# Attention rows from columns by a unit matrix, maxima three heads ahead, GpSimd's last bias after the columns

## The chip, the cores and the metric

The kernel runs on one core of a Trainium2 chip. The metric is the device time of one execution in microseconds. Three runs of the kernel before gave 1441.47, 1442.12 and 1445.12 us; their median is 1442.12.

## The reference

Five blocks, each with a residual and a layer norm where the reference has them, work on 625 nodes with 768 features and 10,000 edges. The first two (relational and plain graph convolution) are untouched. The change concerns the graph attention layers, all of this form:

```python
def gat(x, W, a_src, a_dst, bias, src, dst, heads, c):
    h = (x @ W).reshape(n, heads, c)
    al_s, al_d = einsum(h, a_src), einsum(h, a_dst)      # one number per node and head
    e = leaky_relu(al_s[src] + al_d[dst], 0.2)
    e = exp(e - segment_max(e, dst)[dst])
    alpha = e / (segment_sum(e, dst)[dst] + 1e-16)
    return segment_sum(h[src] * alpha, dst) + bias
```

There are four: a residual block with 4 heads of 256 (layer A, `Q0`) and 1 head of 768 (layer B, `Q1`), both with self loops, and a block with 8 heads of 96, then ELU (`Q2`), and 1 head of 768 (`Q3`), whose output gets the residual and the last layer norm.

## The kernel before, in words

Edges are held as dense count matrices of 625 by 625, in 5 blocks of 125 nodes. Every engine has its own program, written out by hand in order; they meet only by counting semaphores. TensorE multiplies features and weights in split precision: a block of work is 3 products (high by low, low by high, high by high). The weights come in chunks of 128 rows, which ScalarE splits into a high part and GpSimd into the rest (`split_hi`, `split_to`).

A feature product has two pieces of 384 columns. The first piece also gives each node's two attention numbers, `al`. The second runs block by block (`chunks_and_scores`, 30 blocks, 40 in layer B), and a table of events (`PAIR_EVENTS`) says before which block TensorE does something for the scores. For a head h:

1. `turn_scores` (once a layer) turns `al` into rows; ScalarE copies them.
2. `send_row` gives every partition the row of source numbers in banks 5 and 6, or 2 and 3.
3. `largest`, five times: VectorE adds the mask of a block and takes the maximum.
4. `columns`: six small VectorE operations make, for each destination, the two numbers of leaky relu minus maximum, "steep" and "flat", each as a high and a low part (`row_parts`).
5. `turn_columns`: five TensorE turns make rows of them; `keep_columns`: ScalarE copies these in two operations.
6. `send_columns`: products with a stationary operand of two ones give every partition the flat and the steep row (with one pad column, 626).
7. `keep_flat`: ScalarE copies the flat row to SBUF; the steep row stays in PSUM.
8. `score`, five times on VectorE: the larger of steep row plus source number and flat row. ScalarE takes the exponential, `finish` on VectorE multiplies by the counts. In heads 1 to 7 of the eight-head layer the last three tiles (`LATE = 3`) go to ScalarE in two steps each and to GpSimd for the counts (`late_products`).
9. `sum_head` (or `sum_tile`): TensorE sums the features with these tiles.

In the eight-head layer the second piece is followed by a loop over the heads. TensorE, in turn h: row of head h+2, send of head h+1, sum of head h, turn of head h+2's columns. VectorE: inverse of head h-1, products of head h, maxima and columns of head h+2, scores of head h+1. ScalarE: the read of head h-1, flat row and exponentials of head h+1, ELU of head h-1. GpSimd: late products of head h+1, bias of head h, ELU sum of head h-1. In front of the last head TensorE turns the first half of the next layer's input. In the last layer GpSimd adds the bias to the residual (`x_residual`, five operations, L1046) as soon as its row is loaded.

Lines: `largest` L2204, `columns` L2213 to L2221, `score` L2253, `finish` L2260, inverse L2271 and L2273, `turn_columns` L2968, `send_columns` L2980, `send_row` L2960, `sum_head` L3061, the last layer's sums L3033 (first block) and L3011, `keep_flat` L1321, late products L1019, layer B's additions L974 (GpSimd) and L2317 (VectorE).

## Time and profile before

| | us |
|---|---|
| median of three runs | 1442.12 |
| profiled execution, its own time | 1445.38 |
| its span, first to last instruction | 1443.5 |
| TensorE busy | 1373.3 (95%) |
| VectorE busy | 775.4 (54%) |
| GpSimd busy | 548.4 (38%) |
| ScalarE busy | 445.3 (31%) |

Times in rows are microseconds from the start of the span. The second piece of layer B runs from about 1115 to 1139, that of the eight-head layer from 1241 to 1260, its heads from there to 1358, the second piece of the last layer from 1376 to 1401, and its sums to the end. Busy time of TensorE counts pipelined products by their whole duration, so a line of 0.34 us can follow the one before it by 0.18 us. `[5.72 <-ACT ...]` behind a row is the idle time before it and who ended it. In the names POOL is GpSimd, ACT ScalarE, DVE VectorE, PE TensorE.

### The profile page before, as it was taken

Reading aid. Unit: us, or ns where it says so; the run is one execution under the profiler, and the core shown is the slowest. Engines: PE = TensorE matmul, PEld = TensorE weight load, DVE = VectorE, ACT = ScalarE, POOL = GpSimd, SP = SyncE. Lnnn points to the kernel's source line nnn. Section 1 sums busy time; section 2 is a strip of 40 time slices with the busy share of each in tenths; the row PEclk is TensorE's granted clock in tenths of the full one; section 3 lists DMA queues with packets and bytes.
Section 4 is the critical chain, followed back from the end, with each engine's and each line's share of the span. In section 5 each row is a group of like instructions: output and inputs, shape, how many; then the busy total and the mean of one; then the engine's idle time right before and its main releaser. Section 6 shows DMA issues by size and latency. Waiting matters only on the chain.

```text
span 1443.5 us, 22327 instructions
## 1 busy us (share of the span) xinstructions
PE 1373.3 (95%) x7674; PEld 1275.8 (88%) x7674; DVE 775.4 (54%) x1843; ACT 445.3 (31%) x953; POOL 548.4 (38%) x626
## 2 busy tenths in 40 slices
PE   5999999999999999999999999999999999878997
PEld 3676999999999999999999999999978976767974
DVE  7876755234444356573232535764464615499554
ACT  1564521111100010110110312244574434557631
POOL 8000325234253434434342443144333654427630
PEclk9999999999999999999999999999999999977999
DMA  3101111113343223241121211122001311200001
GB/s 117 55 29 34 39 34 55 44 39 113 95 119 92 66 93 110 82 140 58 55 66 33 88 45 51 44 88 78 29 23 44 110 44 39 77 1 1 1 11 54
DMA packets 57802, 86.47 MB, mean 60 GB/s; under 512 B 6467, under 2 KB 54458, under 8 KB 57583
## 3 DMA queue, kind: packets, MB, share of 16 engines
q1 hardware_dynamic: 45204, 65.82, 15.3%
q10 hardware_dynamic: 12504, 19.36, 4.4%
q8 instruction: 63, 1.03, 0.3%
q14 instruction: 31, 0.25, 0.1%
HBM read 83.24 MB, written 1.92 MB: 59 GB/s over the span
## 4 chain that ended last, share of the span: by engine, by line
PE 79%; DVE 12%; ACT 3%; issue 2%; POOL 2%; DMA 1%; DVEq 0%; SPq 0%; ACTq 0%; POOLq 0%
PE psum L2499 13%; PE psum L2503 13%; PE psum L2502 13%; PE psum L2516 7%; PE psum L2519 7%; PE psum L3011 5%; DVE max_scratch L2204 3%; PE psum L2648 3%; PE psum L2573 2%; PE psum L3061 2%; PE psum L2912 1%; PE psum L2542 1%; PE psum L2545 1%; PE psum L2916 1%; PE psum L2917 1%
## 5 line engine op out<-in xcount | busy, mean ns | idle before, releaser
L2499 PE MATMUL psum<-w_lo,xT_hi 128*125 128x384 f32 (+4 forms) x1110 | 377.5, 340 | 3.8 <-POOL w_lo L926 1.8
L2503 PE MATMUL psum<-w_hi,xT_hi 128*125 128x384 f32 (+4 forms) x1110 | 373.4, 336 | 0.0
L2502 PE MATMUL psum<-w_hi,xT_lo 128*125 128x384 f32 (+4 forms) x1110 | 373.3, 336 | 0.0
L913 POOL CAST w_hi<-w_raw 128x384 fp32r<-128x384 f32 x190 | 105.1, 553 | 569.6 <-PE psum L2503 466.0
L1098 ACT ACTIVATE h_hi<-psum 125x384 fp32r<-125x384 f32 (+1 forms) x120 | 59.1, 492 | 529.3 <-PE psum L2503 524.9
L1754 DVE TENSOR_TENSOR h_lo<-psum,h_hi 125x384 fp32r<-125x384 f32 (+1 forms) x120 | 67.0, 558 | 286.6 <-ACT h_hi L1098 285.8
L2499 PEld LDWEIGHTS psum<-w_lo,xT_hi 128*125 128x125 f32 (+1 forms) x1110 | 205.9, 186 | 6.5 <-POOL w_lo L926 3.4
L915 POOL TENSOR_TENSOR w_lo<-w_raw,w_hi 128x384 fp32r<-128x384 f32 x190 | 201.1, 1059 | 15.2
L2502 PEld LDWEIGHTS psum<-w_hi,xT_lo 128*125 128x125 f32 (+1 forms) x1110 | 206.4, 186 | 0.4
L2503 PEld LDWEIGHTS psum<-w_hi,xT_hi 128*125 128x125 f32 (+1 forms) x1110 | 206.0, 186 | 0.0
L2516 PE MATMUL psum<-h_lo,adjacency 125*125 125x384 f32 (+3 forms) x600 | 203.5, 339 | 2.1 <-issue 1.9
L2519 PE MATMUL psum<-h_hi,adjacency 125*125 125x384 f32 (+3 forms) x600 | 202.8, 338 | 0.0
L926 POOL TENSOR_TENSOR w_lo<-w_raw,w_hi 128x384 fp32r<-128x384 f32 x86 | 89.7, 1074 | 92.4 <-ACT w_hi L1295 92.4
L2516 PEld LDWEIGHTS psum<-h_lo,adjacency 125*125 125x125 f32 (+1 forms) x600 | 111.4, 186 | 3.1 <-issue 2.7
L2519 PEld LDWEIGHTS psum<-h_hi,adjacency 125*125 125x125 f32 (+1 forms) x600 | 111.7, 186 | 0.0
L3011 PE MATMUL psum<-features,score_tiles 125*125 125x257 f32 (+2 forms) x380 | 107.6, 435 | 0.0
L3011 PEld LDWEIGHTS psum<-features,score_tiles 125*125 125x125 f32 x380 | 70.5, 189 | 27.8
L1936 DVE CUSTOM_DVE_ANT_0 score_products<-score_w_raw,score_a_rows 128x384 f32<-128x384 f32 (+2 forms) x116 | 57.5, 541 | 7.1 <-DMA score_w_raw<-weights_dram 3.4
L1897 DVE SCALAR_TENSOR_TENSOR x_nat<-psum,inv_degrees,x_nat 125x384 f32<-125x384 f32 x100 | 54.3, 610 | 11.8 <-PE psum L2519 11.7
L1701 DVE TENSOR_SCALAR onehot_dst<-iota,dst_of_sweep 128x625 bf16<-128x625 f16 x132 | 47.3, 395 | 13.8 <-PE psum L2648 13.7
L2648 PE MATMUL psum<-onehot_dst,onehot_src 128*125 128x512 bf16 (+1 forms) x264 | 49.2, 326 | 3.8 <-DVE onehot_dst L1701 2.8
L2648 PEld LDWEIGHTS psum<-onehot_dst,onehot_src 128*125 128x125 bf16 x264 | 31.2, 146 | 21.7 <-issue 15.3
(358 smaller groups left out, 2263.0 us busy)
## 6 DMA issues: line engine op xcount, KB each, us to landing
w_raw<-weights_dram SPq DMA_DIRECT2D x296, 192.0 KB, 2.4
score_w_raw<-weights_dram ACTq DMA_DIRECT2D x58, 192.0 KB, 2.9
x_nat<-x_dram SPq DMA_DIRECT2D x1, 1875.0 KB
x_residual<-x_dram SPq DMA_DIRECT2D x5, 375.0 KB
score_a_rows<-L_gnn_a_src_dram ACTq DMA_DIRECT2D x8, 192.0 KB, 3.6
score_a_rows<-L_gnn_a_dst_dram ACTq DMA_DIRECT2D x8, 192.0 KB, 4.8
out_dram<-x_residual SPq DMA_DIRECT2D x4, 375.0 KB
rgcn_bias<-rgcn_bias_dram SPq DMA_DIRECT2D x1, 1125.0 KB
```

The source lines that it names most:

```text
L913: nc.gpsimd.tensor_copy(mem.wh[:, slot, :], mem.raw[:, raw_slot, :]).then_inc(w_hi_ready, 1)
L915: nc.gpsimd.tensor_tensor(mem.wl[:, slot, :], mem.raw[:, raw_slot, :], mem.wh[:, slot, :].bitcast(F32), ALU.subtract).then_inc(w_lo_ready, 1)
L926: nc.gpsimd.tensor_tensor(mem.wl[:, c % WRING, :], mem.raw[:, c % RAW, :], mem.wh[:, c % WRING, :].bitcast(F32), ALU.subtract).then_inc(w_ ...
L1098: nc.scalar.activation(mem.hh[0:p, slot, 0:HW], bank(ring_bank(u), 0, HW, p), ACT.Copy).then_inc(h_hi_ready, 1)
L1754: nc.vector.tensor_tensor(o, p, h, ALU.subtract).then_inc(h_lo_ready, 1)
L2499: ins = nc.tensor.matmul(o, h, wl, start=(j == 0), stop=False, skip_group_check=True)
L2502: nc.tensor.matmul(o, l, wh, start=False, stop=False, skip_group_check=True)
L2503: ins = nc.tensor.matmul(o, h, wh, start=False, stop=stop and j == k - 1, skip_group_check=True)
L2516: ins = nc.tensor.matmul(o, a, mem.hl[0:p, slot, 0:width], start=(s == 0), stop=False, skip_group_check=True)
L2519: ins = nc.tensor.matmul(o, a, mem.hh[0:p, slot, 0:width], start=False, stop=(s == NB - 1), skip_group_check=True)
L2648: ins = nc.tensor.matmul(o, sources, mem.oh_dst[:, n % OH_RING, w:w + 512 if w == 0 else NC], start=False, stop=(t == GROUP - 1), skip_gro ...
L3011: ins = nc.tensor.matmul(bank(q.out_bank(u), 0, width), p, feat_flat(q, k, a, a + width), start=(k == 0), stop=(k == NB - 1), skip_group_c ...
```

## The change

Steps 5 and 6 are replaced: `send_columns` multiplies the columns themselves, spread over 125 columns as the stationary operand, by a unit matrix (`mem.unit`), once for the high and once for the low part, for each of five blocks and of two rows: 20 products of 125 by 126 where there were 5 turns, 2 copies and 4 products. The rows lie in blocks of 128 columns, and `keep_flat` and `score` read them so. Head 0 of the eight-head layer uses banks 4 to 6 instead of 2 to 4 for its pair, so that the row of the next head can follow.

The events move: scores, row and send before blocks 3, 6 and 16 (before: 4, 8, turn 21, send 24); in the eight-head layer before 2, 5 and 26, with the rows of heads 1 and 2 before 14 and 23. Maxima run three heads ahead, and the columns of head h+2 stand in front of the last score of head h. Head 0 also gives its last three tiles to GpSimd. ScalarE's copy of the flat row and exponentials of the first head move ahead of the feature reads (`EXPS_AHEAD`: all five in layer B, two in the last). GpSimd's bias for the last layer waits for the last layer's columns.

```diff
-PAIR_EVENTS = {4: (("scores", 0),), 8: (("row", 0),), 21: (("turn", 0),), 24: (("send", 0),)}
+PAIR_EVENTS = {3: (("scores", 0),), 6: (("row", 0),), 16: (("send", 0),)}
+HEAD_EVENTS = {2: (("scores", 0),), 5: (("row", 0),), 14: (("row", 1),), 23: (("row", 2),), 26: (("send", 0),)}
...
+        EXPS_AHEAD = [(), range(NB), (), range(2)]
...
+            late_products(0)
             for h in range(LAST):
                 late_products(h + 1)
...
             pool.wait_ge(params_loaded, 16 * 9)
+            pool.wait_ge(cols_ready, Q3.head0 + 1)
             for m in range(NB):
                 r = mem.xres[0:BP, m, :]
...
-                            keep_columns(q, 0)
+                            if not q.by_head:
+                                keep_flat(q, 0)
+                            for k in EXPS_AHEAD[q.index]:
+                                source_exp(q, 0, k)
...
-                    elif piece == 1 and q.index:
-                        if m == 0:
-                            keep_flat(q, 0)
-                        elif m == 2:
-                            source_exp(q, 0, 0)
-                        elif m == NB - 1:
-                            for k in range(1, NB):
-                                source_exp(q, 0, k)
+                    elif piece == 1 and q is Q2 and m == 2:
+                        keep_flat(q, 0)
+                    elif piece == 1 and q is Q3 and m < NB - len(EXPS_AHEAD[3]):
+                        source_exp(q, 0, len(EXPS_AHEAD[3]) + m)
...
+            def head_scores(h):
+                for k in range(NB):
+                    if k == NB - 1 and h + 2 < HEADS3:
+                        columns(Q2, h + 2)
+                    score(Q2, h, k)
             scores_of(Q2, 0)
-            for k in range(NB):
-                score(Q2, 0, k)
             scores_of(Q2, 1)
+            maxima(Q2, 2)
+            head_scores(0)
             for h in range(HEADS3):
                 if h:
                     head_z(h - 1)
-                for k in range(NB - LATE if h else NB):
+                for k in range(NB - LATE):
                     finish(Q2, h, k)
-                if h + 2 < HEADS3:
-                    scores_of(Q2, h + 2)
+                if h + 3 < HEADS3:
+                    maxima(Q2, h + 3)
                 if h + 1 < HEADS3:
-                    for k in range(NB):
-                        score(Q2, h + 1, k)
+                    head_scores(h + 1)
...
             def send_columns(q, h):
 
-                pe.wait_ge(cols_kept, q.head0 + h - HEADS2 + 1)
+                pe.wait_ge(cols_ready, q.head0 + h + 1)
                 if h:
                     pe.wait_ge(tile_scored, scored(q, h - 1, NB - 1))
+                if q.by_head and h < 2:
+                    pe.wait_ge(gemm_read, q.gemm0 + NB + 2 + h)
                 for i in (1, 0):
-                    for p, e, a, z in score_pieces(pair_col(q, h, i), N + 1):
-                        ins = nc.tensor.matmul(ps[0:BP, p:e], mem.both_parts[0:4, i:i + 1].to_broadcast([4, BP]),
-                                               kept_columns(h)[:, a:z], start=True, stop=True)
+                    for m in range(NB):
+                        for part in range(2):
+                            row = mem.row_parts[0:BP, 2 * part + i, m, h:h + 1]
+                            ins = nc.tensor.matmul(pair_row(q, h, i)[:, m, 0:BP + 1], row.to_broadcast([BP, BP]),
+                                                   mem.unit[0:BP, 0:BP + 1], start=(part == 0), stop=(part == 1))
...
             for h in range(HEADS3):
-                if h + 2 < HEADS3:
-                    send_row(Q2, h + 2)
+                if h + 3 < HEADS3:
+                    send_row(Q2, h + 3)
                 if h < LAST:
                     send_columns(Q2, h + 1)
                 sum_head(h, 0, NB)
-                if h + 2 < HEADS3:
-                    turn_columns(Q2, h + 2)
```

## Rows read from the trace of the kernel before

**Rows 1.** The page: busy totals, and the chain's shares.

```profile
PE 1373.3 (95%) x7674; PEld 1275.8 (88%) x7674; DVE 775.4 (54%) x1843; ACT 445.3 (31%) x953; POOL 548.4 (38%) x626
...
PE 79%; DVE 12%; ACT 3%; issue 2%; POOL 2%; DMA 1%; DVEq 0%; SPq 0%; ACTq 0%; POOLq 0%
```

**Rows 2.** Stretches: length, busy PE, PEld, DVE, ACT, POOL, granted clock, DMA share, GB/s.

```profile
1294.45:1306.38 11.93, 9.13 (x60) 8.57 (x60) 11.59 (x26) 8.93 (x19) 8.42 (x7) 0.79 0.00 0
```

**Rows 3.** Timeline of VectorE, one head: start, us, engine, line, form, count.

```profile
1301.48 3.19 DVE L2253 SCALAR_TENSOR_TENSOR score_tiles<-psum,al_src_steep,score_tiles 125x625 f32<-125x625 f32 x4
...
1305.58 0.81 DVE L2260 SCALAR_TENSOR_TENSOR score_tiles<-score_tiles,counts_all 125x625 f32<-125x625 f32 x1
1306.30 0.81 DVE L2204 CUSTOM_DVE_ANT_0 max_scratch<-psum,mask_plain 125x625 f32<-125x625 f32 x1
...
1310.54 0.89 DVE L2213 TENSOR_TENSOR al_sum<-al_max,al 125x5 f32<-125x5 f32 x1
...
1312.63 1.65 DVE L2253 SCALAR_TENSOR_TENSOR more_tiles<-psum,al_src_steep,score_tiles 125x625 f32<-125x625 f32 x2
```

**Rows 4.** Timeline of GpSimd and ScalarE in the same head.

```profile
1305.99 2.79 POOL L1019 TENSOR_TENSOR score_tiles<-score_tiles,counts_wide 125x625 f32<-125x625 f32 x2 [3.43 <-ACT score_tiles L1339]
...
1309.87 0.67 ACT L1321 ACTIVATE score_tiles<-psum 125x625 f32<-125x625 f32 x1
```

**Rows 5.** Timeline of VectorE and GpSimd in head 7.

```profile
1351.59 1.90 DVE L2260 SCALAR_TENSOR_TENSOR score_tiles<-score_tiles,counts_all 125x625 f32<-125x625 f32 x1
...
1351.18 3.46 POOL L1019 TENSOR_TENSOR score_tiles<-score_tiles,counts_wide 125x625 f32<-125x625 f32 x2 [0.88 <-ACT score_tiles L1339]
```

**Rows 6.** Timeline of VectorE: first maximum and columns, scores of heads 0, 1, 5, 7.

```profile
1246.38 0.81 DVE L2204 CUSTOM_DVE_ANT_0 max_scratch<-psum,mask_plain 125x625 f32<-125x625 f32 x1 [3.75 <-PE psum L2960]
...
1251.54 0.18 DVE L2221 TENSOR_TENSOR row_parts<-row_steep_flat,row_parts 125x10 fp32r<-125x10 f32 x1
1257.44 3.97 DVE L2253 SCALAR_TENSOR_TENSOR more_tiles<-psum,al_src_steep,score_tiles 125x625 f32<-125x625 f32 x5 [5.72 <-ACT score_tiles L1321]
...
1277.13 3.19 DVE L2253 SCALAR_TENSOR_TENSOR score_tiles<-psum,al_src_steep,score_tiles 125x625 f32<-125x625 f32 x4
...
1325.36 3.19 DVE L2253 SCALAR_TENSOR_TENSOR score_tiles<-psum,al_src_steep,score_tiles 125x625 f32<-125x625 f32 x4
...
1347.22 3.19 DVE L2253 SCALAR_TENSOR_TENSOR score_tiles<-psum,al_src_steep,score_tiles 125x625 f32<-125x625 f32 x4
```

**Rows 7.** Timeline of TensorE: four fifths of the sum of head 7.

```profile
1353.54 4.61 PE L3061 MATMUL psum<-features,score_tiles 125*125 125x97 f32 x40 [0.32 <-DVE score_tiles L2260]
```

**Rows 8.** Stretches, TensorE alone: length, busy, granted clock, DMA.

```profile
1303.00:1304.60 1.60, 0.00 (x0) 0.96 0.00 0
...
1304.60:1311.00 6.40, 6.35 (x26) 0.50 0.00 0
```

**Rows 9.** Timelines of the last layer: TensorE, VectorE, GpSimd.

```profile
1381.15 0.69 PE L2960 MATMUL psum<-al_rows,row_select 2*125 2x512 f32 x3
...
1391.90 0.69 PE L2968 MATMUL psum<-ident,row_parts 125*4 125x125 f32 x5 [2.96 <-DVE row_parts L2221]
...
1402.01 7.34 PE L3033 MATMUL psum<-features,score_tiles 125*125 125x385 f32 x20 [0.63 <-issue]
...
1386.23 1.57 DVE L2213 TENSOR_TENSOR al_sum<-al_max,al 125x5 f32<-125x5 f32 x1
...
1382.33 8.98 POOL L1046 TENSOR_TENSOR x_residual<-x_residual,par 125x768 f32<-125x768 f32 x5
```

**Rows 10.** Timelines of layer B: TensorE, VectorE, GpSimd.

```profile
1140.05 0.44 PE L2499 MATMUL psum<-w_lo,x8T_hi 128*125 128x384 f32 x1 [0.99 <-ACT features L1375]
...
1144.00 11.03 DVE L2317 TENSOR_TENSOR features<-features,par 125x768 f32<-125x768 f32 x5
...
1146.72 11.81 POOL L974 TENSOR_TENSOR x_residual<-x_residual,par 125x768 f32<-125x768 f32 x5
```

**Rows 11.** TensorE's waits from 1128 to 1175: total, times, longest.

```profile
PE psum L2499 <- POOL w_lo L926: 0.6, 3, 0.2
```

More of the change, by code:

```diff
@@ L154, in pair_bank @@
     def pair_bank(self, h):
-        return 5 if self.residual else 4 if self.by_head and h else 2
+        return 5 if self.residual else 4 if self.by_head else 2
     def out_bank(self, u):
         return u % self.out_banks
-PAIR_EVENTS = {4: (("scores", 0),), 8: (("row", 0),), 21: (("turn", 0),), 24: (("send", 0),)}
+PAIR_EVENTS = {3: (("scores", 0),), 6: (("row", 0),), 16: (("send", 0),)}
+HEAD_EVENTS = {2: (("scores", 0),), 5: (("row", 0),), 14: (("row", 1),), 23: (("row", 2),), 26: (("send", 0),)}
 Q0 = Attention(None, HEADS2, C2, KC, PIECES1, True, BASE_L2, True,
@@ L1543, in head_read, with head_exps @@
                 ins.then_inc(part_read, 1)
-            keep_columns(Q2, 1)
+            def head_exps(h):
+                for k in range(NB - LATE):
+                    source_exp(Q2, h, k)
+                source_below(h, NB - LATE)
+                for k in range(NB - LATE, NB):
+                    if k + 1 < NB:
+                        source_below(h, k + 1)
+                    source_exp_below(h, k)
+            head_exps(0)
             for h in range(HEADS3):
@@ L1553, in _ @@
                     keep_flat(Q2, h + 1)
-                if h + 1 < HEADS3:
-                    for k in range(NB - LATE):
-                        source_exp(Q2, h + 1, k)
-                    source_below(h + 1, NB - LATE)
-                    if h + 2 < HEADS3:
-                        keep_columns(Q2, h + 2)
-                    for k in range(NB - LATE, NB):
-                        if k + 1 < NB:
-                            source_below(h + 1, k + 1)
-                        source_exp_below(h + 1, k)
+                    head_exps(h + 1)
                 if h:
@@ L2260, in finish, with maxima, scores_of @@
                 nc.vector.scalar_tensor_tensor(t, t, 1.0, cnt[0:BP, k, 0:N], ALU.min, ALU.mult).then_inc(tile_ready, 1)
-            def scores_of(q, h):
+            def maxima(q, h):
                 for m in range(NB):
                     largest(q, h, m)
+            def scores_of(q, h):
+                maxima(q, h)
                 columns(q, h)
@@ L2427, in _ @@
                     head_z(h - 1)
-                for k in range(NB - LATE if h else NB):
+                for k in range(NB - LATE):
                     finish(Q2, h, k)
-                if h + 2 < HEADS3:
-                    scores_of(Q2, h + 2)
+                if h + 3 < HEADS3:
+                    maxima(Q2, h + 3)
                 if h + 1 < HEADS3:
-                    for k in range(NB):
-                        score(Q2, h + 1, k)
+                    head_scores(h + 1)
             for n in range(NB):
@@ L3055, in sum_head @@
                 for k in range(first, end):
-                    if h and k >= NB - LATE:
+                    if k >= NB - LATE:
                         pe.wait_ge(late_ready, made_late(h, k))
@@ L3077, in turn_x3 @@
                     pe.wait_ge(layer_ready, NB + 4)
[L3078 removed]
+                    pe.wait_ge(max_done, (Q2.head0 + HEADS3) * NB)
                     if n >= 2:
@@ L3096, in events @@
                             send_row(q, h)
-                        elif what == "turn":
-                            turn_columns(q, h)
                         else:
```

57 lines of the change are left out of this document (14 added, 43 removed).

## The prediction, made before the change was run

> **What bounds the kernel now.** I read the busy totals and the chain of waits on the page first. TensorE is busy for 95% of the span and holds 79% of the chain, VectorE holds 12% [rows 1]. So the question is which stretches TensorE does not bound, and the change touches three: the scores of the second layer of the residual block (one head, I call it layer B), the eight-head layer, and the last layer.
>
> In the eight-head layer the table of stretches shows VectorE busy 11.59 of 11.93 us of a head, TensorE 9.13 [rows 2]: VectorE is the bound. From head 3's scores to head 5's, 1301.48 to 1325.36, a head costs 11.94 us [rows 3, 6]. Its timeline of one head [rows 3] gives the parts. The five scores take 4.0 us (0.80 each). The inverse and two products with counts take 1.8 us (to the start of the maxima at 1306.30). Five maxima take 4.24 us (1306.30 to 1310.54). The six small operations of the columns take 2.09 us (1310.54 to 1312.63), because the first took 0.89. In the first head the same six ended at 1251.72, 1.1 us after the maxima that began at 1246.38 [rows 6]. So a head pays 1.0 us for something that happens on GpSimd beside it.
>
> What that is, rows 5 show. A VectorE product with counts that needs 0.80 us took 1.90 while two GpSimd products took 3.46 instead of the usual 2.79 [rows 4, 5]: a VectorE operation on two SBUF tensors and a GpSimd operation take turns (the maxima, PSUM and one mask, kept 0.81 beside GpSimd [rows 3, 4]). In the last layer three of the small operations each sat out one bias addition of GpSimd, 8.98 us for five: the first took 1.57 us [rows 9].
>
> **The change, part by part.**
>
> *Unit matrix.* Five turns, two copies on ScalarE and four products give way to 20 products, 125 by 126. The nearest row is the sum of a head: 40 instructions with a 125-column weight load in 4.4 us, 0.11 each at full clock [rows 7]; at the lower level (granted 0.50, 1.2 GHz, for 6.4 us after TensorE had been idle [rows 8]) twice that. So a send is 2.2 us, or 4.4 at 1.2 GHz, against 1.3 before (the five turns take 0.45, the four products 0.8). Bounds: 384 columns go through in 0.175 us, a third of that is 0.06, so 1.2 us a send; a two-pass product is two instructions, 4.4 us. I take 2.2, as the load has the same size.
>
> The Trainium skill, "TensorE: Matmul & The Clock Gate", section LDWEIGHTS, has a weight load cost its columns divided by 1.2 in ns; 125 columns then give 104 ns, an estimate of 2.1 us a send. By its gap formula for 126 columns alone it would be 1.1 us. The spacing of 0.11 us in rows 7 sides with the load.
>
> In the eight-head layer this is hidden: a send starts when the last score of a head is done, and VectorE has 6.0 us of other work (1.8 + 4.24) until it needs the rows. Without that cover, in heads 6 and 7, ScalarE's copy is later anyway. Reading the rows through 128-column blocks I cost at 0 (as many elements; bounds 0 to 0.1 a score, 0.5 a head).
>
> *Start of the eight-head layer.* The row event moves from block 8 to 5 of the second piece, 1.6 us at 0.53 a block, so the first maximum starts at 1244.8 instead of 1246.38 [rows 6]. Three rounds of maxima (12.7) and two of columns (2.2, up to 1 more beside weight splits) now fill what was a 5.72 us gap: first score at 1260.5 instead of 1257.44. With columns(2) in between, the scores of head 0 end at 1265.7. Two products (1.5, three went to GpSimd), maxima of head 3 (4.25), then scores and columns (5.1): the scores of head 1 end at 1276.6, against 1280.3. Gain 3.7. The send of head 1 starts on an idle TensorE at 1265.7; even at 4.4 us it is done at 1270.1, before 1271.5.
>
> *Middle of it.* A head keeps the same VectorE work; only the order is new. Let S be the first score. Columns now run at S+3.2, when GpSimd is between heads (its products began at S+5.3 before, 1305.99 against 1300.7, one score before 1301.48 [rows 3, 4]; without the column copies of 0.6 us on ScalarE at S+4.7). That gives 1.0 back. But the scores then end at S+5.1, and the two products with counts come at S+5.4, when GpSimd's first product runs (S+4.7 to 6.0). The first waits 0.6. GpSimd's second asks at S+6.6, the first ends at about S+6.7. If VectorE keeps the turn, a head is 11.75 us; if GpSimd gets it as in rows 5, the second product waits 1.4 more and a head is 13.15. So four heads (1 to 5) cost between 47.0 and 52.6 against 47.8. Middle: 12.4, a loss of 1.8 (I take it because nothing shown settles the turn).
>
> *End of it.* Heads 6 and 7 have no maxima between. The next score waits for ScalarE's copy of the flat row, S+9.2 before [rows 4]; by its queue S+9.9, then S+9.3. So from the end of head 5's scores to head 7's it is 9.9 - 5.1 + 9.3 + 4.0 = 18.1 us, against 21.9 before (1328.5 to 1350.4 [rows 6]). Gain 3.8. After head 7 nothing changes its distance. The layer gains 3.7 - 1.8 + 3.8 = 5.7 (2.9 to 8.5).
>
> *Last layer.* Row at block 6 instead of 8: 1380.1 for 1381.15 [rows 9]. Maxima end at 1385.1, and the columns, with GpSimd held back, at 1386.2 instead of 1391.8. The send stands at block 16, about 1386.1 (13 blocks took 7.1 us before the stall, 1381.8 to 1388.9 [rows 9]), so the 2.96 us stall goes; 2.2 us later TensorE resumes and ends its blocks at 1396.0. But the five bias additions (9.0 us) start at 1386.2 and now meet the products with counts, from 1391.2: each of the first three sits out a piece of one. Scores go on at 1392.6, 1395.2 and 1397.8, the last at 1398.6. ScalarE has put its last exponentials ahead of the last two feature copies, so these end at 1400.3, and the sum starts there, not at 1402.01. The gap of 4.3 us is longer than the idle one in front of the lower clock of rows 8, so I let the clock fall again; that costs the sum (7.34 us before, 6.5 at full clock: 20 products of 385 or 384 columns at 0.32) about 2.8: end at 1409.6 against 1409.2. I take 0; bounds -5 (no such waiting: the sum starts at 1397.6, at full clock) and +1.5.
>
> *Layer B.* The send moves to block 16, where the columns (2.7 us beside weight splits) are not ready: stall 1.9, send 2.2, and TensorE is 2.0 late at the end of the piece. There it waited 0.99 us for ScalarE's copies [rows 10]; with ScalarE's exponentials in front the residual products start 1.6 late. ScalarE also sends the last gain row's load 2.1 later or more, and GpSimd's additions wait for it. But those took 11.81 us for five, 1.8 each without company [rows 9], as VectorE's five additions of 11.03 ran beside them [rows 10]; those will be over first, which pays for the delay. TensorE's own waits for split weights, 0.6 us [rows 11], vanish. Net +1.0; bounds +0.3 and +3.
>
> **Sum.** +1.0 - 5.7 + 0 = -4.7 us. The profiled execution took 1445.38 us, so it would take 1440.7; the median shown is 1442.12, which the same difference takes to 1437.4.
>
> The Trainium skill, "SBUF — State Buffer", section "SBUF: two separate sides", says that the pair of ports shared by VectorE and GpSimd is an exclusive lock, held for a whole instruction, and that a VectorE operation with two SBUF inputs takes it. It speaks against this change: the columns leave the lock and the products with counts enter it, which is the mechanism of rivals 2 and 3. Rows 5 agree with it.
>
> **Rivals.**
> 1. *The lock stays out of it.* VectorE keeps its turn (11.75 a head, layer gain 8.5) and the last layer gains 3 to 5. For it: the margin is 0.1 us either way. Sum +1 - 8.5 - 4 = -11.5: 1430.6.
> 2. *GpSimd wins each turn.* 13.15 a head: gain 2.9, last layer +0.5, layer B +2: -0.4, so 1441.7. For it: rows 5. Against it: a slightly later last score shifts GpSimd's request too.
> 3. *Slower: the lock becomes the period.* If GpSimd's sums of a head slide past S+3.2, columns are caught as well: 13.15 + 1.0 to 2.0, say 14.6. Four heads are 58.4 against 47.8, the ends give back 7.5: +3.1; layer B +2.5, last layer +1: +6.6, 1448.7. The layer turns to a loss above 13.9 us a head ((47.8 + 7.5 + 0.3)/4). Against it: GpSimd ends a head's work near S+14.6, which at 13.15 is S+1.5 of the next.
> 4. *The send is dearer.* Load and product not overlapped, or 1.2 GHz throughout: above 6.0 us a send VectorE waits. At 1.2 GHz it is 4.4, so only a factor of 2.7 on rows 7 does it; then it joins rival 3.
>
> **Chances.** A measurement of this kernel tells about 0.3% (4.3 us) from no change. The forecast, with its own range 1434 to 1440, 0.45, of which half is over the bound; rival 1 0.27; rival 2 0.2; rivals 3 and 4 together 0.08. Faster by over 0.3% 0.50 (half of the forecast's and rival 1), within 0.42 (the other half and rival 2), slower 0.08. The range reaches from rival 1 past rival 2: 1428 to 1443.5.
>
> **What would show it.** In the changed trace: 20 instructions per send spaced 0.11 us at full clock; first score of the eight-head layer near 1260.5 (plus layer B's 1.0); columns of 1.1 us in heads 2 to 5 and, behind them, products with counts of 1.4 or 2.2 us where 0.8 stood; heads at 12.4 apart; heads 6 and 7 at 9 to 10. In the last layer small operations at 0.17 us, no stall at the send, products with counts near 1.5 us beside the bias additions, and a gap of about 4 us before the sum with a granted clock of 0.5 behind it. It is wrong if the products with counts keep 0.8 us (then rival 1), if a send costs over 6 us, or if the residual products of layer B start more than 3 us late.

## The result, and the profile after

The changed kernel took 1450.73 us (median of 6, 1448.37 to 1456.83); the kernel before, beside it, 1444.36 us (median of 6). The ratio is 1.0035, 95% interval 1.0019 to 1.0052: slower by about 5 us, where 4.7 us faster was forecast, and outside the stated 1428 to 1443.5. The profiled execution took 1448.37 us (span 1446.6), 3.0 us more than the one of before. It is the fastest of its six, so the trace accounts for 3.2 us of span; what makes the median a further 2 to 3 us slower, no trace shows.

The page of the changed kernel, busy totals and the chain's shares:

```profile
PE 1380.5 (95%) x7784; PEld 1286.7 (89%) x7784; DVE 770.4 (53%) x1839; ACT 442.7 (31%) x936; POOL 555.9 (38%) x629
...
PE 75%; DVE 14%; ACT 3%; issue 3%; POOL 2%; DMA 1%; DVEq 0%; SPq 0%; ACTq 0%; POOLq 0%
```

Beside [rows 1] the chain has moved from TensorE (79 to 75%) towards VectorE. The totals hardly tell where; starts of the same instruction in both traces do. Each stretch below is the difference of two starts, in us.

| stretch | before | after |
|---|---|---|
| layer B: ScalarE's last copy of `al` to the first sum | 56.37 | 62.81 |
| to the first maximum of the eight-head layer | 75.17 | 73.62 |
| to the first score of head 7 | 100.05 | 99.66 |
| to the last layer's first product | 11.50 | 11.21 |
| to the last layer's first sum | 44.08 | 41.86 |
| that sum (20 products), to the next | 7.18 | 9.42 |

They add up to +4.2. The profiled execution of the changed kernel came 1.05 us earlier into layer B, where nothing had yet been changed, and +3.2 is left, the difference of the spans. Layer B alone cost 6.4 us. TensorE in layer B, changed kernel:

```profile
1123.20 0.34 PE L2913 MATMUL psum<-w_hi,x8T_hi 128*125 128x384 f32 x1
1125.54 4.46 PE L2966 MATMUL psum<-unit,row_parts 125*125 125x126 f32 x20 [2.00 <-DVE row_parts L2208]
1129.79 0.63 PE L2908 MATMUL psum<-w_lo,x8T_hi 128*125 128x384 f32 x1
1130.22 0.52 PE L2912 MATMUL psum<-w_hi,x8T_lo 128*125 128x384 f32 x1
```

The stretches around it, TensorE alone (length, busy, granted clock, DMA share, GB/s):

```profile
1118.00:1125.40 7.40, 5.54 (x31) 1.00 0.57 162
1125.50:1132.00 6.50, 6.46 (x27) 0.50 0.17 56
1132.00:1143.00 11.00, 11.00 (x64) 0.99 0.26 80
```

A wait of 2.00 us, and behind it the clock stood at its lower level (0.50, 1.2 GHz) for 6.5 us: the send took 4.46 us and a chunk product 0.52. From there TensorE works without a gap up to the residual products, which begin at 1143.89. Counted from the copy of `al` (at 1113.79, before at 1114.84), that is 30.10 us where it was 25.21 [rows 10]: 4.9 us of the 6.4 are lost by then, and 1.5 behind (32.71 us to the first sum for 31.16). ScalarE and GpSimd in the same place:

```profile
1130.03 0.69 ACT L1308 ACTIVATE score_tiles<-psum 125x625 f32<-125x625 f32 x1 [6.61 <-PE psum L2966]
1130.74 1.28 ACT L1314 ACT_TABLE_LOAD   x1
1132.04 2.95 ACT L1314 ACTIVATE score_tiles<-score_tiles,al_src_slope 125x625 f32<-125x625 f32 x4
...
1135.60 2.17 ACT L1292 ACTIVATE w_hi<-w_raw 128x384 fp32r<-128x384 f32 x5
1141.79 0.53 ACT L1292 ACTIVATE w_hi<-w_raw 128x384 fp32r<-128x384 f32 x1 [4.03 <-DMA w_raw<-weights_dram]
...
1142.78 0.26 ACTq L1281 DMA_DIRECT2D par<-L_gnn_g_dram  x1
```

```profile
1152.95 1.84 POOL L985 TENSOR_TENSOR par<-par,par0b 125x768 f32<-125x768 f32 x1 [8.78 <-DMA par<-L_gnn_g_dram]
1154.88 9.05 POOL L969 TENSOR_TENSOR x_residual<-x_residual,par 125x768 f32<-125x768 f32 x5
```

ScalarE waits 6.61 us for the send with five raw weight chunks queued behind it, and makes the exponentials before it splits them. It then waits 4.03 us for the chunk after those. TensorE had split weights enough all the same: it shows no wait for them before 1144. The gain row's load is issued at 1142.78 (1138.06 before) and used at 1152.95 (1144.77 before). GpSimd's five additions did take 9.05 us instead of 11.81, as forecast, but began 8.2 us later. TensorE's waits from 1128 to 1180 (total, times, longest), to set against [rows 11]:

```profile
PE psum L2495 <- POOL w_lo L921: 1.1, 6, 0.2
```

The eight-head layer, VectorE: the columns of head 0 beside GpSimd's weight splits, the first scores of heads 1, 2 and 3 (1278.37, 1292.92, 1305.48) and what lies between.

```profile
1254.48 0.64 DVE L2200 TENSOR_TENSOR al_sum<-al_max,al 125x5 f32<-125x5 f32 x1
1255.16 0.92 DVE L2201 SCALAR_TENSOR_TENSOR al_max<-al_sum 125x5 f32<-125x5 f32 x1
...
1257.39 0.92 DVE L2208 TENSOR_TENSOR row_parts<-row_steep_flat,row_parts 125x10 fp32r<-125x10 f32 x1
...
1278.37 0.87 DVE L2240 SCALAR_TENSOR_TENSOR more_tiles<-psum,al_src_steep,score_tiles 125x625 f32<-125x625 f32 x1
...
1285.43 0.17 DVE L2263 TENSOR_SCALAR z<-psum 125x5 f32<-125x5 f32 x1 [2.11 <-PE psum L3047]
...
1292.92 3.19 DVE L2240 SCALAR_TENSOR_TENSOR more_tiles<-psum,al_src_steep,score_tiles 125x625 f32<-125x625 f32 x4
...
1298.09 3.34 DVE L2248 SCALAR_TENSOR_TENSOR more_tiles<-more_tiles,counts_all 125x625 f32<-125x625 f32 x2
...
1305.48 0.87 DVE L2240 SCALAR_TENSOR_TENSOR more_tiles<-psum,al_src_steep,score_tiles 125x625 f32<-125x625 f32 x1
...
1308.59 0.17 DVE L2200 TENSOR_TENSOR al_sum<-al_max,al 125x5 f32<-125x5 f32 x1
```

In the middle heads the small operations of the columns are at 0.17 us, and the two products with counts take 3.34 instead of 1.5: the lock (a VectorE and a GpSimd operation taking turns, as in rows 5) moved as forecast, and a head takes 12.56 us (12.4 forecast, 11.94 before). Not forecast is the 2.11 us wait of head 0's inverse for TensorE's sum; the step from head 1 to head 2 takes 14.55 us. The sum ran at the lower clock, behind a gap and a slow send (a later one takes 5.65 us at full clock):

```profile
1272.98 4.43 PE L2966 MATMUL psum<-unit,row_parts 125*125 125x126 f32 x20 [3.13 <-DVE row_parts L2208]
1277.21 8.19 PE L3047 MATMUL psum<-features,more_tiles 125*125 125x97 f32 x50
```

The last layer, TensorE and its stretches:

```profile
1389.53 2.40 PE L2966 MATMUL psum<-unit,row_parts 125*125 125x126 f32 x20
...
1402.95 9.58 PE L3019 MATMUL psum<-features,score_tiles 125*125 125x385 f32 x20 [3.51 <-DVE score_tiles L2248]
```

```profile
1398.00:1400.00 2.00, 1.44 (x9) 1.12 (x7) 2.00 (x3) 1.09 (x2) 1.79 (x1) 1.00 0.00 0
1400.00:1402.00 2.00, 0.00 (x0) 0.00 (x0) 1.96 (x3) 0.83 (x3) 0.00 (x0) 0.99 0.00 0
1402.00:1404.00 2.00, 1.05 (x2) 0.77 (x3) 0.81 (x1) 1.98 (x4) 0.00 (x0) 0.50 0.00 0
1404.00:1408.00 4.00, 4.00 (x7) 2.05 (x7) 0.00 (x0) 0.15 (x1) 0.00 (x0) 0.50 0.00 0
```

The stall at the send is gone [rows 9], and TensorE reaches its sum after a gap of 3.51 us; the clock falls as the sum starts, and the 2.2 us won are spent on it.

### The profile page after: what moved, and what is told of

It reads as the page before. It is cut to its first block, busy times and chain, and to the rows that moved or that the text cites. A ratio compares the mean times of both kernels' runs of the same rounds, so it can differ in the third digit from the quotient of the medians.

```text
span 1446.6 us, 22524 instructions
## 1 busy us (share of the span) xinstructions
PE 1380.5 (95%) x7784; PEld 1286.7 (89%) x7784; DVE 770.4 (53%) x1839; ACT 442.7 (31%) x936; POOL 555.9 (38%) x629
## 3 DMA queue, kind: packets, MB, share of 16 engines
q8 instruction: 64, 1.05, 0.3%
## 4 chain that ended last, share of the span: by engine, by line
PE 75%; DVE 14%; ACT 3%; issue 3%; POOL 2%; DMA 1%; DVEq 0%; SPq 0%; ACTq 0%; POOLq 0%
PE psum L2495 13%; PE psum L2499 13%; PE psum L2498 13%; PE psum L2512 7%; PE psum L2515 7%; PE psum L2997 5%; DVE max_scratch L2191 3%; PE psum L2644 2%; PE psum L2569 2%; DVE onehot_dst L1688 1%; PE psum L2538 1%; PE psum L2541 1%; POOL w_lo L921 1%; PE psum L2484 1%; DVE more_tiles L2240 1%
## 5 line engine op out<-in xcount | busy, mean ns | idle before, releaser
L2265 DVE RECIPROCAL z<-psum 125x1 f32<-125x1 f32 x25 | 4.2, 166 | 89.2 <-PE psum L2997 89.2
```

## Experiments

All ratios are to the kernel before, run beside them on the same chip, with 95% intervals. Where two medians are subtracted, both kernels ran on one chip. A stretch is read from one profiled execution. Code is given in short.

**Layer B: the send later.** `16: (("send", 0),)` becomes 21 for this layer.

> The changed kernel, but in layer B alone the twenty products that send the rows are issued five chunk blocks later (in front of block 21 of that layer, not 16). Stall theory: most of what layer B lost is TensorE's 2.00 us wait for the split columns (1125.54, 20 products at 4.46 us) and what follows from it, the granted clock of 0.50 for the send (4.46 us where 2.2 was expected) and for the eight products behind it (about 1 us). Five blocks are 5 x 0.53 = 2.65 us of work, more than the 2.00 us of the wait: the send starts without a gap at full clock, takes 2.2 us, and the layer's last products (residual product) begin about 5 us earlier than 1143.89. Median 5 us below the changed kernel's (1445 to 1447), ratio to the kernel before 0.999 to 1.001. Rival, ScalarE's queue: what was lost comes from keeping the flat rows and five exponentials (with the 1.28 us table load) ahead of the splits and of the loads of the gain row; these stay where they are, so the time stays within 1 us of the changed kernel's, ratio 1.003, or grows since they come later still.

Measured 1.0046 [1.0024, 1.0067]: no gain in time, although the trace's stretch is 1.8 us shorter. TensorE of this run:

```profile
1143.66 0.44 PE L2495 MATMUL psum<-w_lo,x8T_hi 128*125 128x384 f32 x1 [3.88 <-ACT features L1362]
```

The gap at the send is gone, and a new one of 3.88 us stands in front of the residual products, for ScalarE's features, again with a low clock behind it (0.62 and 0.53 from 1144 to 1148). The stall theory alone does not give the time back.

**Flat rows and exponentials behind.** In layer B, with the send at 16:

```
-    for k in EXPS_AHEAD[1]: source_exp(Q1, 0, k)   # and keep_flat ahead of it
+    m == 0: keep_flat; m == 2: source_exp 0; m == NB - 1: source_exp 1 to 4
```

> The changed kernel, but in layer B alone ScalarE keeps the flat rows after the first block of features of the second half, makes the first exponential after the third and the other four after the fifth, as in the kernel before; the send stays in front of block 16. Stall theory: TensorE still waits 2.00 us and the send still takes 4.46 us at half clock; only the 1 to 1.6 us of late splits (chunks 0.97 us apart where 0.53 is usual) can come back. Time 0 to 1.5 us below the changed kernel's, ratio to the kernel before 1.0025 to 1.0035. Rival, ScalarE's queue: the splits of the raw chunks start at 1130 instead of 1135.6, the three row loads are issued about 4 us earlier, GpSimd's additions start at about 1148 instead of 1152.95 and the splits behind them are in time; then the 5 us come back here, ratio 0.999 to 1.001.

Measured 1.0063 [1.0048, 1.0078], slower than either expected. ScalarE goes on splitting while it would have waited for the send, GpSimd splits the low halves beside VectorE's columns, and five of these six small operations take 0.6 to 1.0 us (three in the changed kernel). The send's gap grows.

```profile
1126.83 4.46 PE L2974 MATMUL psum<-unit,row_parts 125*125 125x126 f32 x20 [3.60 <-DVE row_parts L2216]
```

**Both edits.** 

> Both edits together: the send of layer B in front of block 21, and keeping the flat rows and the exponentials behind the features. Stall theory: as the send alone, or 0 to 1.5 us better: 1444 to 1446, ratio 0.998 to 1.001. If the two causes lie one behind the other and each is real, this is below both single edits by the smaller of their two gains. If ScalarE's queue is all of it, this equals the second edit alone.

Measured 1.0015 [0.9996, 1.0034]; the stretch is 59.46 us. The columns come 0.97 us too late even at block 21.

**The loads first.** The three `load_row` calls of the layer go ahead of `keep_flat`.

> The changed kernel, but in layer B ScalarE issues its three row loads (bias, shift, gain: 375 KB each) one behind the other before it keeps the flat rows and makes the exponentials; nothing else moves. Stall theory with the late splits as its smaller part: the gain row is in at about 1145 instead of 1152.95, GpSimd's six additions (10.9 us) end near 1156 or, beside VectorE's bias additions at 1144.4, near 1158, its splits of the low halves are in time, and TensorE's chunk waits of the second half of the residual product vanish: 1 to 1.6 us below the changed kernel's, ratio 1.002 to 1.003. Rival, the loads' lateness is the main cost: 4 to 5 us, ratio 0.999 to 1.001. Or the 1.1 MB of row loads together hold back the raw chunks that the same 16 DMA engines bring, and the time stays or grows by 1 us.

Measured 1.0015 [1.0002, 1.0028]; the stretch of layer B is 59.73 instead of 62.81 us. Up to the residual products it is the same (29.85 for 30.10); behind them it is 29.88 for 32.71. So the late rows were worth 3.1 us, more than the 1 to 1.6 I gave them and less than the rival's. GpSimd is at the gain row at 1146.50 here.

**Send at block 24, exponentials behind.** Both edits, with 24 instead of 21.

> The changed kernel with layer B's work put back into the order of the kernel before: the send in front of block 24, the flat rows kept and the exponentials made behind the feature copies of the second half. Against the kernel with both moved but the send at block 21 (ratio 1.0015), only the send is 1.6 us later; there the columns came 0.97 us after TensorE had run dry and the granted clock fell to 0.50 for some 3 us. Theory of two limits one behind the other (the send's gap with its clock, and ScalarE's queue): with neither, the stretch from the last copy of the columns' products to layer B's first sum is 57.4 us, the 56.4 us of the kernel before and the 1.0 us of the forecast; 5.4 us less than in the changed kernel (62.8). Median ratio to the kernel before 0.998 to 1.001. Rival: what remains of the loss lies behind layer B (eight-head layer, last layer), then it stays at 1.0015 or above.

Measured 0.9991 [0.9977, 1.0004], median 1444.57 us. The stretch is 56.71 us, 0.3 above before.

Two more with the send at 24 tell ScalarE's two edits apart. **Flat rows kept ahead, exponentials behind:**

> The changed kernel, in layer B with the send in front of block 24 and the exponentials behind the feature copies, but the flat rows kept ahead of the second half's splits, as the change has it. Exponentials theory: what starves TensorE is the 5.0 us of table load and exponentials that stand between the send and the next five splits; without them the splits follow 0.7 us after the send's end, and the stretch from the last copy of the columns' products to layer B's first sum is 57 to 58.5 us (56.7 with both behind): ratio to the kernel before 0.999 to 1.001. Keep theory: ScalarE already stands at the send (6.61 us idle in the changed kernel) with splits queued behind it, and the later send makes that wait longer: the stretch is 60 us or more, ratio 1.0015 or above.

**Both ahead, as the change has them:**

> The changed kernel with the send of layer B in front of block 24 and nothing else moved: flat rows and all five exponentials stay ahead of the splits. With the send in front of block 21 TensorE had no gap before the send and then stood still for 3.88 us at 1139.8, because the splits came after the exponentials. Both theories: three blocks (1.6 us) later ScalarE's chain, and with it the splits, come 1.6 us later still, TensorE has three blocks less to do behind the send, and its stall grows to 5 to 6 us: the stretch up to the first sum is 62.5 to 64.5 us, ratio 1.003 to 1.006. If the send's gap were the cause, this would be as fast as with everything put back (0.999).

Measured 0.9998 [0.9981, 1.0015] and 1.0032 [1.0015, 1.0049], on one chip. TensorE stood still for 5.28 us in the second:

```profile
1144.30 0.68 PE L2495 MATMUL psum<-w_lo,x8T_hi 128*125 128x384 f32 x1 [5.28 <-ACT features L1362]
```

Nine kernels on layer B, stretch from the traces:

| send at block | flat rows kept | exponentials | stretch, us |
|---|---|---|---|
| 24 (before) | behind | behind | 56.37 |
| 24 | behind | behind | 56.71 |
| 24 | ahead | behind | 57.69 |
| 24 | ahead | ahead | 62.69 |
| 21 | behind | behind | 59.46 |
| 21 | ahead | ahead | 61.03 |
| 16 | behind | behind | 64.73 |
| 16 (changed) | ahead | ahead | 62.81 |
| 16, loads first | ahead | ahead | 59.73 |

Either edit alone costs nearly the whole loss of 6.4 us or more: exponentials ahead cost 5.0 us with the send at 24, the early send 8.0 with the exponentials behind. They are two limits side by side, and taking one away shows the other. That is why the first run measured nothing.

**GpSimd's wait.** On the kernel with the send at 24, without `pool.wait_ge(cols_ready, Q3.head0 + 1)`.

> As the run with the send in front of block 24, without GpSimd's wait for the last layer's columns in front of its five bias additions (9 us): they run at once, beside the maxima and the columns, as in the kernel before. Theory (the wait only moves the lock, from the columns, 1.57 us for the first of them, to the products with the counts, 1.6 us each instead of 0.8): within 1 us of the run without this edit, ratio to it 1.000 give or take 0.001. Rival, the wait is worth what the change's name says: without it columns come 1 to 2 us later and the send starts after a longer gap of TensorE: 1.5 to 3 us slower. Other rival: the products free of the lock give the last sum 2 to 3 us sooner at full clock: 2 to 3 us faster.

Measured 1.0025 [1.0008, 1.0042], 3.6 us above the median with the wait. My theory falls; the first rival holds in kind and is exceeded in size (1.5 to 3 us). VectorE's columns and TensorE's send of this run (its profiled execution is 9.5 us above its median, so rows are read here, not its span):

```profile
1394.93 0.27 DVE L2207 TENSOR_TENSOR al_sum<-al_max,al 125x5 f32<-125x5 f32 x1
1395.23 1.74 DVE L2208 SCALAR_TENSOR_TENSOR al_max<-al_sum 125x5 f32<-125x5 f32 x1
1397.01 1.72 DVE L2209 TENSOR_TENSOR row_steep_flat<-al,al_max 125x5 f32<-125x5 f32 x1
...
1398.84 1.66 DVE L2214 CAST row_parts<-row_steep_flat 125x10 fp32r<-125x10 f32 x1
...
1400.77 4.46 PE L2973 MATMUL psum<-unit,row_parts 125*125 125x126 f32 x20 [4.79 <-DVE row_parts L2215]
```

5.8 us for what takes 1.1: three of the six small operations each sit out one of GpSimd's additions. The cast has a single SBUF input; it waits too. TensorE then stands still for 4.79 us in front of the send, where the changed kernel has no wait. The Trainium skill, "SBUF — State Buffer", section "SBUF: two separate sides", says that the loser of the shared ports is blocked for the whole instruction; the trace agrees (three waits of 1.5 us beside additions of 1.8).

**Two heads ahead.** Maxima and columns of the eight-head layer in the order of the kernel before (head 0's scores ahead of head 1's maxima, head 1's row behind the chunks), rows still by the unit matrix:

```
-                if h + 3 < HEADS3: maxima(Q2, h + 3)      # columns in front of the last score
+                if h + 2 < HEADS3: scores_of(Q2, h + 2)   # maxima and columns together
```

> As the run with the send in front of block 24, and in the eight-head layer maxima and columns two heads ahead as in the kernel before (row 1 behind the chunks, row h+2 in front of the send for head h+1, columns of head h+2 right behind its maxima, in front of the five scores); rows still by the unit matrix, head 0's last three tiles still multiplied by GpSimd. Theory: the changed kernel's eight-head layer gained 2 us over before, and what gained was that the maxima and columns of heads 1 and 2 stand ahead of the scores of head 0 and the columns lie out of the lock; then this is 2 to 4 us slower than the run without this edit, ratio 1.001 to 1.003. Rival: the gain is the unit matrix (no transposes, no ScalarE copies, no waits on them), and three heads ahead only moved the lock onto the products with the counts (12.6 us a head against 11.94): then this is 2 to 5 us faster than without the edit, ratio 0.995 to 0.998.

Measured 1.0052 [1.0032, 1.0072], 9.2 us above the median with three ahead: the theory's sign, at over twice its size (2 to 4 us). Heads 2 to 6 alternate between 12.0 and 14.6 us. TensorE's clock is low in the short heads (0.63 and 0.52) and high in the long ones (0.95 and 0.92). From head 1's first score to head 7's it is 78.9 us, against 70.1 in the kernel before. In this order, then, the rest of the change makes the layer slower; three heads ahead is what pays for it. Why every second head is longer was not taken apart.

**Head 0's products on VectorE.** 

> The run with the send in front of block 24 (ratio 0.9991), with head 0 of the eight-head layer multiplied by the counts on VectorE alone, five tiles instead of two, as in the kernel before. Theory: GpSimd's part in head 0 takes three products of 0.8 us off VectorE, in front of head 1's scores' maxima; but head 1's inverse waited 2.11 us for the sum of head 0, which ran at half clock. With all five on VectorE (2.4 us more there, no lock with GpSimd) the heads behind start 0 to 2.4 us later: ratio 0.999 to 1.001. Rival: head 0's products by GpSimd cost the lock in head 0 (two products at 1.09 and 2.12 us) and make the sum late; then this is equal or up to 2 us faster: 0.9975 to 0.999.

Measured 1.0007 [0.9986, 1.0028]: unclear in time. The trace shows two effects that cancel: head 1's scores begin 2.2 us later (30.31 us behind the first maximum, 28.15 in the changed kernel), the inverse no longer waits for TensorE, and head 2's scores stand where they stood (42.93 for 42.70).

**The products with the counts behind the maxima.** In VectorE's order, with TensorE summing GpSimd's three tiles first:

```
+                if h + 3 < HEADS3: maxima(Q2, h + 3)
                 for k in range(NB - LATE): finish(Q2, h, k)
-                if h + 3 < HEADS3: maxima(Q2, h + 3)
```

> As the run with the send in front of block 24, and in the eight-head layer VectorE makes the five maxima of three heads on before its two products with the counts, and TensorE sums the three tiles that GpSimd multiplies before the two of VectorE. Lock theory: of the 12.6 us a head some 1.8 us are VectorE's two products (3.3 us a pair where 1.53 were needed in head 3) while GpSimd multiplies three tiles; behind the maxima (4.25 us) they find GpSimd in the bias strip, and a head takes 11 to 11.6 us in the five heads that have maxima: 4 to 6 us below the run without this edit, ratio to the kernel before 0.995 to 0.997. Rival, TensorE: its sum of a head then waits 3 to 4 us for VectorE's tiles, the granted clock falls to 0.50, 50 products take 8 us instead of 5.9, and the inverse of that head, which VectorE does first in the next one, waits for it: no gain, or 1 to 4 us slower than without the edit.

Measured 0.9976 [0.9966, 0.9987], median 1442.89 us, 1.7 below the run without the edit (4 to 6 expected). One head as a stretch (columns as in [rows 2]), first of the run without the edit, then with it:

```profile
1305.12:1317.67 12.55, 11.75 (x98) 11.30 (x98) 12.24 (x26) 8.52 (x16) 8.85 (x7) 0.96 0.00 1
```

```profile
1299.70:1311.85 12.15, 12.15 (x97) 11.90 (x96) 11.00 (x26) 8.52 (x16) 8.82 (x7) 0.89 0.01 1
```

VectorE's wait in the lock is gone from this head (12.24 to 11.00 us busy), but the head falls by 0.4 only: TensorE, with its clock at 0.89, is busy throughout, and the inverse waits 0.60 us for it. Theory and rival both acted. The eighth head lost 1.5 us (12.75 from its first score to the last layer, 11.22 without).

**That order for heads 0 to 4 only.** 

> The run with the products with the counts behind the maxima, but TensorE sums GpSimd's tiles first only for the five heads that have maxima beside them; for heads 5 to 7 it takes the tiles in the old order. In that run the eighth head took 12.75 us from its first score to the last layer's first product, against 11.22 without the edit, since GpSimd's tiles, made last, were waited for first. Theory: these 1.5 us come back, heads 0 to 4 stay at 12.1 us: 1 to 2 us below that run, ratio to the kernel before 0.9963 to 0.9970. Rival: in heads 5 and 6 the order of the tiles decides nothing, and the 1.5 us were spent waiting for GpSimd's chain in either order: same as that run, 0.9976 give or take 0.001.

> The kernel with layer B in the old order, the products with the counts behind the maxima, and GpSimd's tiles first in heads 0 to 4, timed again beside the one with the early sum: 0.9975 to 0.9995 of the kernel before (0.9995 [0.9979, 1.0012] and, with all heads GpSimd first, 0.9976 [0.9966, 0.9987] on other chips).

Measured 0.9995 [0.9979, 1.0012] and, again, 0.9986 [0.9966, 1.0005] on another chip. The trace gives the 1.5 us back (11.21); in time it can't be told from the run before.

**Products in the gap before the last sum.**

```
+    for _ in range(8):    # 16 in the second run
+        nc.tensor.matmul(ps[0:BP, 5 * 512:6 * 512], mem.row_sel[0:2, 0:1].to_broadcast([2, BP]), mem.al_T[0:2, 0:512], ...)
```

> The previous run, and eight more products of 512 columns on TensorE in the last layer, into a bank nobody reads, between the send and the first sum, from the moment the first feature block of the second half is copied (about 2.6 us after the send's end). In the changed kernel TensorE idles for some 11 us there with a granted clock of 1.00, and the clock falls to 0.50 only when the sum begins (windows 1400 to 1410: 0.70 and 0.62), so that its 20 products take 9.58 us against 7.34; in the kernel before it fell to 0.50 in 1395 to 1400, where TensorE had nothing to do, and the sum ran at 0.99 to 1.00. Clock theory: it is work after a gap that brings on the slow clock, for some 6.5 us of time; eight cheap products bring it on early, the sum of the last layer then takes 7.3 us: 1.5 to 2.5 us below the previous run, ratio about 0.0013 lower. Rival: the sum is slow because of its own waits for tiles, and more work adds to it: no change or up to 1 us slower.

> As the run with eight more products, with sixteen: at the slow clock they take 6.8 us and fill the gap up to the sum. Clock theory: if what brings the full clock back is time (6.5 us) after work has begun again, sixteen do the same as eight, and the sum takes 7.3 us; if it is the amount of work done, eight are not enough and sixteen are. Either gain is 1.5 to 2.5 us against the run without them; if the sixteen run past the start of the sum, up to 0.7 us of it is lost.

Measured 0.9990 [0.9972, 1.0009] and 0.9999 [0.9985, 1.0013], and 0.9995 without them on the same chip: nothing. The expectation misread the gap: 14 chunk blocks lie between send and sum, and TensorE idles 3.5 us, not 11. It also had the kernel before idle while its clock was low; there TensorE was busy for the whole of 1394 to 1398, at 0.50. The eight took 2.11 us at full clock, from 3.56 us before the sum. The sixteen took 3.96, not 6.8, and filled the gap to its end, and the sum still took 8.39 us:

```profile
1392.00:1394.00 2.00, 2.00 (x10) 1.50 (x9) 2.00 (x3) 0.88 (x2) 0.57 (x1) 1.00 0.00 0
1394.00:1396.00 2.00, 2.00 (x10) 1.33 (x8) 1.55 (x3) 1.93 (x4) 0.00 (x0) 1.00 0.00 0
1396.00:1398.00 2.00, 2.00 (x4) 1.16 (x4) 0.00 (x0) 0.93 (x1) 0.00 (x0) 0.51 0.00 0
```

**The last sum begins early.** Its banks are 5 and 6 instead of 0 and 1, and it waits block by block:

```
-                    pe.wait_ge(gemm_read, q.gemm0 + NB * len(q.pieces))
+                    pe.wait_ge(gemm_read, q.gemm0 + NB + max(2, k + 1))   # for tile k
```

> The kernel of the run that follows, and in the last layer the first sum goes to banks 5 and 6 instead of 0 and 1 and waits for each node block's features by itself, not for all of them: it may begin when two of the five copies are made. In the run before, the sum began at 1394.63, 0.1 us behind ScalarE's last feature copy, while the first three tiles had been ready for some 2 to 6 us. Theory: the order in which ScalarE makes exponentials and copies sets the sum, not the columns; now four of the five parts are done by the time of the last copy, and the first sum ends 3 to 6 us sooner: 2.5 to 6 us below the same kernel without the edit, ratio about 0.996. Rival: what remains behind the last copy runs at the slow clock for 6.5 us in any case, and half of the gain is lost: 1.5 to 2.5 us.

Measured 0.9936 [0.9913, 0.9958], median 1436.16 us, 5.4 below the same kernel without the edit beside it. TensorE and its stretches:

```profile
1393.95 6.62 PE L3028 MATMUL psum<-features,score_tiles 125*125 125x385 f32 x20
```

```profile
1394.00:1396.00 2.00, 2.00 (x8) 1.19 (x7) 2.00 (x3) 0.84 (x3) 0.46 (x1) 1.00 0.00 0
1396.00:1398.00 2.00, 2.00 (x8) 1.19 (x7) 1.43 (x2) 1.98 (x4) 0.00 (x0) 1.00 0.00 0
1398.00:1400.00 2.00, 2.00 (x7) 1.14 (x7) 0.03 (x1) 0.81 (x1) 0.00 (x0) 1.00 0.00 0
```

The sum follows the last chunk block with no gap, the clock stays at 1.00, and it takes 6.62 us. It starts 3.6 us earlier behind the layer's first product (38.25 us for 41.85) and is 1.8 us faster, which together is the 5.4. This version, which also has layer B put back and the products behind the maxima, beats both kernels: 9 us below before, and by the ratios (0.9936 and 1.0035) some 14 below the change.

## Why the prediction was wrong, step by step

Two terms of the sum fail: layer B, +6.4 us for +1.0, and the eight-head layer, -2.2 for -5.7. The last layer came out.

*What bounds.* Right: VectorE in the eight-head layer, lock included.

*Unit matrix.* Right: 2.30 to 2.40 us a send at full clock (2.2), 4.16 to 4.46 behind a gap (4.4 at the lower clock).

*Layer B: the step that failed.* I wrote "Net +1.0; bounds +0.3 and +3"; it was +6.4. The stall was right (1.9 forecast, 2.00 measured). The send that stands behind it was priced at 2.2, at full clock, although rows 8 and the last layer's step had the clock fall behind gaps. It took 4.46, and the half clock went on over the chunk products behind it: 2.3 us for the send and about 1.2 for those (an estimate: 2.4 us at half clock). With them the 1.6 forecast for the start of the residual products becomes 5.1, and 4.9 was measured, past the 3 us that I had named as a sign of being wrong. The rest lies behind: TensorE's 0.6 us of waits for split weights were to vanish, and that part grew by 1.5 us. The gain row, taken as "2.1 later or more", was used 8.2 us later (9.2 counted from the copy of `al`), and "which pays for the delay" failed; with the loads first this part is 2.8 us shorter. ScalarE's exponentials in front of five splits cost nothing that the changed kernel's trace shows before the residual products; they are the second limit, worth 5.0 us once the send stands later. With everything in the old order the stretch costs 0.3, the lower bound.

*Start of the eight-head layer: mis-sized, 2.4 for 3.7.* The first maximum comes 1.6 us earlier, as forecast, and head 1's scores end 33.1 us behind it (33.9 before, 31.8 forecast). The term too small is the columns beside weight splits: head 0's took 3.75 us (1254.48 to 1258.23) and head 1's 1.3, where 2.2 and "up to 1 more" stood for both. The first score came 17.70 us behind the first maximum, not 15.7.

*Middle: mis-sized, -4.0 for -1.8.* The period was right, 12.56 for 12.4, with products of 3.34 a pair, but for three heads of the four. The first took 14.55. I let TensorE's send of head 1 take its 4.4 us, but not the 50 products of head 0 behind it at the same clock, 8.19 us, for which head 0's inverse waits 2.11 us.

*End.* Right: from the end of head 5's scores to head 7's it is 18.3 us for 18.1, and 0.3 less after that. So the layer gained 2.2 us where 5.7 was forecast.

*Last layer.* Right as a sum: 0.0 for 0. Columns uncontended, no stall, products with counts of up to 1.68 us beside the bias additions, a gap, the clock down and the sum at 9.58 us. Its parts are larger than the zero lets one think: GpSimd's wait alone is worth 3.6, and the late start of the sum with its clock costs 5.4, as the early sum shows.

*Rivals.* "Slower" had a chance of 0.08, and rivals 2 and 3 raised layer B to 2 and 2.5 us, but none named a mechanism in it. Rival 3's period of 14.6 us did appear, in every second head of the kernel with two heads ahead. The bounds of the layer's gain are 2.7 and 8.3 by their own terms, not 2.9 and 8.5; nothing hangs on it. With layer B put back (0.9991, -1.3 us, give or take 2, of which layer B is +0.3) the other terms together give about -1.6 us for -5.7; the trace's stretches say -2.2.

Argued and not shown is the path by which the exponentials hold TensorE up, through late splits and raw slots that come free late. A wait of ScalarE for a chunk (4.03 us) does not show it, since one of 4.46 us stands in the kernel with the send at 24 that loses nothing. Shown is that taking the exponentials out of the way gives 5.0 us back there. Open, too, is why the same instructions ahead of head 0's first score take 17.7 us in twelve of the profiled executions and 20 to 21.4 in four; VectorE's columns there lie beside GpSimd's splits.

## What to carry to other kernels

Before an operation that waits is moved forward in a queue, list what stands behind it there (here five splits and three loads) and price the latest of them, not the nearest. A gap on TensorE can cost itself plus what runs at half the clock behind it, the next engine's wait included; price both. When undoing one of two edits changes nothing, undo both before calling either harmless.

## What the runs showed of the hardware

Behind a gap of 2.00 us the granted clock stood at 0.50 for the next 6.5 us. In the changed kernel it stood at or near 0.50 behind gaps of 3.13, 3.51, 3.57 and 3.86 us too, and at 1.00 behind one of 1.74 (at 1262.49). The length of the gap alone does not settle it: with both edits in layer B (send at 21) a gap of 0.97 us was followed by 0.56 two microseconds later and one of 0.99 by 1.00. Sixteen products of 2 rows by 512 columns kept TensorE busy up to the sum, and the clock still fell to 0.51; chunk products of 128 rows right up to it kept 1.00. ScalarE's table load began 0.02 us after the copy before it had ended, and the first exponential 1.30 us after the load's start (1130.74 to 1132.04), so nothing came on top of the load's 1.28. The Trainium skill, "ScalarE: Activation LUTs", section "What ACT_TABLE_LOAD costs", adds a drain of about 1.38 us to each switch to another set of functions; this trace shows none, and the measurement decides.
